# A Mamba scan and a mixture of experts on one core: the last chunk's serial stage in other PSUM banks, half of the scan's products on GpSimd, and activation tables requested by name

## What is computed

```python
# layer 0: Mamba block, then a small fp8 matmul
xi, res = split(x @ in_proj.T)                      # 256 + 256
xi = silu(causal_conv4(xi))
dt, B, C = split(xi @ x_proj.T, [64, 80])           # 64, 16, 16
delta = softplus(dt @ dt_proj.T + b)
h[t] = exp(delta*A) * h[t-1] + delta*B*u ; y = sum_n h*C + u*D    # 256 channels x 16 states
x = layernorm(x + (y * silu(res)) @ out_proj.T)
x = layernorm(x + fp8(x) @ fp8(w).T + bias)
# layer 1: a scan over 16 states with one step size per token, then the experts
x = layernorm(x + ssm(x))
probs = softmax(x @ Wr); top 2 of 8 experts, at most 512 slots for each expert
contrib = w * ((gelu(rms(x)@Wg[e]) * (rms(x)@Wu[e])) @ Wd[e] + x)    # 128 -> 256 -> 128
out = where(overflow, side_net(x) + x, x + sum(contrib)) ; x = layernorm(out)
```

## Time and profile before

| | us |
|---|---|
| median of 3 runs | 533.24 (530.87 to 534.29) |
| the profiled execution's own time | 535.09 |
| its span, first to last instruction | 533.3 |
| TensorE busy | 425.3 (80%) |
| VectorE busy | 419.7 (79%) |
| ScalarE busy | 315.1 (59%) |
| GpSimd busy | 178.6 (33%) |

### The profile page before, as it was taken

The page is one execution under the profiler, slowest core; times in us unless marked ns, Lnnn a source line. Parts: engine busy times, 40 slices in busy tenths (PEclk is TensorE's granted clock), DMA queues, the critical chain, the costliest instruction groups (busy, mean ns, idle before and its releaser), DMA issues.

```text
span 533.3 us, 5892 instructions
## 1 busy us (share of the span) xinstructions
PE 425.3 (80%) x1680; PEld 256.9 (48%) x1680; DVE 419.7 (79%) x942; ACT 315.1 (59%) x517; POOL 178.6 (33%) x147
## 2 busy tenths in 40 slices
PE   4976667699649999997569999775599995449994
PEld 3322212253235778552245776432367774147883
DVE  3087999997989999698989989978899884334654
ACT  2586552378738976577578785255787832544232
POOL 0056485555163434234163433451534100000000
PEclk9987977799969999999869999969799998656997
DMA  8295768666426354442193554620835000000000
GB/s 300 109 339 175 240 210 263 211 217 202 163 79 200 116 171 161 142 160 78 32 334 133 180 167 132 220 92 20 323 151 175 23 1 1 20 0 1 0 1 20
DMA packets 22064, 74.18 MB, mean 139 GB/s; under 512 B 2320, under 2 KB 4368, under 8 KB 21648
## 3 DMA queue, kind: packets, MB, share of 16 engines
q1 hardware_dynamic: 22032, 73.82, 41.0%
HBM read 72.50 MB, written 1.31 MB: 138 GB/s over the span
## 4 chain that ended last, share of the span: by engine, by line
PE 50%; DVE 21%; issue 13%; ACT 12%; POOL 2%; DVEq 0%; ACTq 0%; POOLq 0%
PE ps_y L475 12%; PE ps_u L608 9%; PE ps_g L564 8%; DVE ps_state L919 6%; PE ps_u L564 5%; DVE product L934 3%; PE ps_state L564 2%; ACT x L703 2%; ACT ps_state L692 2%; DVE stats L944 1%; PE ps_y L608 1%; POOL drive L813 1%; PE ps_g L523 1%; DVE l_state L990 1%; PE ps_g L534 1%
## 5 line engine op out<-in xcount | busy, mean ns | idle before, releaser
L813 POOL TENSOR_TENSOR drive<-du,b_row 128x512 f32<-128x512 f32 x128 | 164.0, 1290 | 208.3 <-DVE ps_state L919 186.0
L475 PE MATMUL ps_y<-product,par 128*128 128x512 f32 x256 | 135.7, 655 | 13.2 <-DVE product L934 12.9
L692 ACT ACTIVATE ps_state<-delta,decay_rate 128x512 f32<-128x512 f32 x128 | 86.2, 687 | 63.9 <-DVE product L934 61.9
L934 DVE TENSOR_TENSOR product<-ps_state,c_row 128x512 f32<-128x512 f32 x128 | 86.1, 680 | 5.5 <-PE ps_y L475 5.3
L919 DVE TENSOR_TENSOR_SCAN ps_state<-ps_state,carry,drive 128x512 f32<-128x512 f32 x64 | 81.5, 1282 | 4.0 <-ACT ps_state L692 4.0
L475 PEld LDWEIGHTS ps_y<-product,par 128*128 128x128 f32 x256 | 48.9, 208 | 70.6 <-issue 37.3
L919 DVE TENSOR_TENSOR_SCAN ps_state<-ps_state,drive 128x512 f32<-128x512 f32 x64 | 77.3, 1219 | 2.3 <-ACT ps_state L692 2.3
L608 PEld LDWEIGHTS ps_u<-wd,hidden 128*128 128x128 f32 x448 | 54.2, 191 | 5.4 <-issue 2.4
L608 PE MATMUL ps_u<-wd,hidden 128*128 128x128 f32 x448 | 54.6, 275 | 0.0
L1092 DVE SCALAR_TENSOR_TENSOR acc<-ps_u,net_weight,acc 128x128 f32<-128x128 f32 x128 | 35.9, 344 | 15.3 <-PE ps_u L608 12.5
L774 ACT ACTIVATE gelu<-ps_g 128x512 f32<-128x512 f32 (+1 forms) x42 | 24.4, 597 | 31.8 <-PE ps_g L564 18.5
(11 more groups left out here) (199 smaller groups left out, 605.4 us busy)
## 6 DMA issues: line engine op xcount, KB each, us to landing
b_row<-bc_dram SPq DMA_DIRECT2D x64, 512.0 KB, 5.0
c_row<-bc_dram SPq DMA_DIRECT2D x64, 512.0 KB, 4.1
x_in<-x_t SPq DMA_DIRECT2D x4, 256.0 KB, 7.0
gelu<-w_gate SPq DMA_DIRECT2D x1, 1024.0 KB, 9.3
hidden<-w_up SPq DMA_DIRECT2D x1, 1024.0 KB, 10.9
wd<-w_down SPq DMA_DIRECT2D x1, 1024.0 KB, 12.8
out<-result SPq DMA_DIRECT2D x4, 256.0 KB, 2.4
par<-params SPq DMA_DIRECT2D x1, 598.0 KB, 6.7
```

Of the source, the lines that this page charges most:

```text
L475: mm(ps_y[:, :], ident, product[:, g % PRODUCTS, :], start=False, stop=(n == STATE - 1)).then_inc(y_pe, 1)
L692: nc.scalar.activation(ps_state[g % RING][:, :], delta[:, c % 2, h, :], ACT.Exp, scale=decay_rate[:, h, n:n + 1]).then_inc(decay_act, 1)
L813: nc.gpsimd.tensor_tensor(drive[:, g % DRIVES, :], du[:, h, :], b_row[:, m % ROWS, n % 2, :], ALU.mult).then_inc(drive_pool, 1)
L934: v.tensor_tensor(product[:, g % PRODUCTS, :], state[:, :], c_row[:, m % ROWS, n % 2, :], ALU.mult).then_inc(product_dve, 1)
```

## The change

It does four things.

1. **Orders.** All lists of `PLACES` are new, one for each chunk, and gate, up and join are placed by half expert (17 places) in place of whole experts (9). On ScalarE and VectorE all 8 splits stand before the scan of chunk 0. VectorE's queue has, between the tail of chunk 0 (its step 1) and the first join of chunk 0, the units 1.4 to 1.21 (chunk.unit); in the MoE of chunk 0 1.22 to 2.4; then 2.5 to 2.12 before step 1 of chunk 1's tail; to its first join 2.13 to 2.28; in the MoE of chunk 1 2.29 to 3.10; then 3.11 and 3.12; and beside the tail of chunk 2 3.13 to 3.31, so all of the scan. On TensorE's queue two units of `finish` remain inside the MoE of chunk 2.
2. **Chunk 3's tail in the banks of the scan.** `tail_bank` gives chunk 3 `ps_state` and `ps_y`, and `l1_of` gives it `product` buffers for its temporaries. Its steps 0 to 11 are placed between the half experts of chunk 2's MoE on all engines. From step 12 (which overwrites the experts' input `hn_parts`) it waits for the last gate and up of chunk 2. `result` becomes an alias of `acc`, so the acc of a chunk is begun only when the result of the chunk before is stored.
3. **Products on GpSimd.** 10 units of chunk 0 (2, 5, ... 29) and the 16 odd units of chunks 1, 2 and 3 are `multiplied`: VectorE's scan writes to `drive` in SBUF in place of the PSUM bank, GpSimd multiplies there and, in chunks 0 and 2, copies the carry column. The bank is free for the next decay when the scan is done. `drive` goes from 5 to 6 buffers, `product` from 5 to 8. (Pairing of products by GpSimd is in the code, but its sets are empty.)
4. **Tables by name.** `use(name)` requests a set only where the set last requested in program order differs. By the new order that is 71 requests. The softplus of pre goes half by half through one `sp_exp` buffer.

The diff, cut to its core (the lists of places are left out; `tail_bank(c, ...)` replaces the banks in all of tail):

```diff
-DRIVES = 5
-PRODUCTS = 5
+DRIVES = 6
+PRODUCTS = 8
+THIRD = frozenset(range(2, UNITS, 3))
+ODD = frozenset(range(1, UNITS, 2))
+MULTIPLIED = (THIRD, ODD, ODD, ODD)
...
+        result = acc
...
+        def l1_of(c, name):
+            name = {"ln": "abs", "t": "sp"}.get(name, name)
+            i = L1_NAMES.split().index(name)
+            if c == CHUNKS - 1:
+                place = product[:, i, :]
...
+        def tail_bank(c, name):
+            if c == LAST:
+                return {"r1": ps_state[0], "x1t": ps_state[1], "ffn": ps_state[2], "x2t": ps_y, "dlt": ps_state[2],
+                        "bx": ps_state[0], "mean": ps_state[1], "r3": ps_y, "hnt": ps_state[2], "logits": ps_state[1],
+                        "counts": ps_y}[name]
...
# tensor
             def tail(c, k):
                 if k == 0:
-                    if c:
+                    if c == LAST:
+                        pe.wait_ge(product_dve, count(by_vector, STEPS - 1))
+                        pe.wait_ge(state_dve, STEPS)
+                    elif c:
...
             def gate(c, i):
                     if c == LAST:
-                        pe.wait_ge(product_dve, STEPS)
+                        pe.wait_ge(hidden_dve, 2 * NETS * c)
+                        pe.wait_ge(gelu_act, 2 * NETS * c)
...
# scalar
+            def use(name):
+                if table[0] != name:
+                    nc.scalar.preload_act_table_set(name)
+                    table[0] = name
...
             def step(c, k):
+                use(EXP_LN)
...
                 if old >= 0:
-                    act.wait_ge(product_dve, old + 1)
-                    if old // UNITS % PER_BATCH == 0:
-                        act.wait_ge(carry_dve, carries(old))
+                    if multiplied(old):
+                        act.wait_ge(state_dve, old + 1)
+                    else:
+                        made(act, old)
...
             def tail(c, k):
                 if k == 12:
+                    if c:
+                        act.wait_ge(gate_pe, 2 * NETS * c)
+                        act.wait_ge(up_pe, 2 * NETS * c)
...
                 if k == 15:
                     if c:
-                        after(act, fin_act, c - 1, "result")
+                        act.wait_ge(stored, 16 * c)
...
# gpsimd
             def step(c, k):
                 if g >= DRIVES:
-                    pool.wait_ge(state_dve, g - DRIVES + 1)
+                    if multiplied(g - DRIVES):
+                        made(pool, g - DRIVES)
...
+            def multiply(c, k):
+                if not multiplied(g):
+                    return
+                pool.wait_ge(state_dve, g + 1)
+                pool.wait_ge(c_in[m % ROWS], 16 * (m // ROWS + 1))
+                if g >= PRODUCTS:
+                    added(pool, g - PRODUCTS)
+                nc.gpsimd.tensor_tensor(product[:, g % PRODUCTS, :], drive[:, g % DRIVES, :], c_row[:, m % ROWS, n % 2, :],
+                                        ALU.mult).then_inc(product_pool, 1)
+                if c % PER_BATCH == 0:
+                    nc.gpsimd.tensor_copy(carry[:, h, n:n + 1], drive[:, g % DRIVES, CHUNK - 1:CHUNK]).then_inc(carry_pool, 1)
...
# vector
             def step(c, k):
-                v.tensor_tensor_scan(state[:, :], state[:, :], drive[:, g % DRIVES, :],
+                v.tensor_tensor_scan(drive[:, g % DRIVES, :] if multiplied(g) else state[:, :], state[:, :], drive[:, g % DRIVES, :],
...
             def finish(c, k):
+                if multiplied(g):
+                    return
```

More of the change, by code:

```diff
@@ L42 @@
 EXP_LN = "natural_log_exp_and_others"
+GELU = "gelu_and_others"
+SILU = "silu_and_others"
 PARAMS = {
@@ L203, in build @@
         product = sb("product", [P, PRODUCTS, CHUNK])
+        def l1_of(c, name):
[3 more added lines that the diff above has]
+                place = product[:, i, :]
+            elif i < 6:
+                place = gelu[:, i // 2, i % 2, :]
+            else:
+                place = hidden[:, 1, 0, :]
+            return place[0:STATE, :] if name in ("step", "decay", "drive") else place
         carry = sb("carry", [P, HALVES, STATE])
@@ L459, in pre @@
                     after(pe, pre_act, c, "low")
-                    last = mm(bank_[:, :], dt_proj[0:RANK, h * P:(h + 1) * P], low[0:RANK, q, :], start=True, stop=True)
+                    last = mm(bank_[:, :], dt_proj[0:RANK, h * P:(h + 1) * P], low[0:RANK, :], start=True, stop=True)
                 last.then_inc(pre_pe.sem, 1)
@@ L821, in tail, with pair @@
                                             ALU.add).then_inc(tail_pool.sem, 1)
-            run("gpsimd", du=make_du, step=step, tail=tail)
+            def multiply(c, k):
+                g = c * UNITS + k
+                h, n = divmod(k, STATE)
+                m = g // 2
+                if not multiplied(g):
[8 more added lines that the diff above has]
+                    nc.gpsimd.tensor_copy(carry[:, h, n:n + 1], drive[:, g % DRIVES, CHUNK - 1:CHUNK]).then_inc(carry_pool, 1)
+            def pair(c, k):
+                g = c * UNITS + k
+                if not paired(g):
+                    return
+                made(pool, g - 1)
+                made(pool, g)
+                nc.gpsimd.tensor_tensor(product[:, g % PRODUCTS, :], product[:, (g - 1) % PRODUCTS, :],
+                                        product[:, g % PRODUCTS, :], ALU.add).then_inc(pair_pool, 1)
+            run("gpsimd", du=make_du, step=step, multiply=multiply, pair=pair, tail=tail)
         @block.vector
@@ L993, in tail @@
+                    if not first:
+                        own(tail_dve, c - 1, "keep")
+                    do(tail_dve, v.tensor_tensor_scan(l1_state[:, :], l1_of(c, "decay"), l1_of(c, "drive"),
+                                                      0.0 if first else l1_carry[:, :], ALU.mult, ALU.add))
+                    own(tail_dve, c, "scan")
+                    do(tail_dve, v.tensor_copy(l1_carry[:, :], l1_state[:, CHUNK - 1:CHUNK]))
                 if k == 9:
                     after(dve, tail_pe, c, "r3")
-                    layer_norm_stats(tail_dve, c, lambda j: block_of(ps_g[0][:, :], j), "st3", "mo3")
+                    layer_norm_stats(tail_dve, c, lambda j: block_of(tail_bank(c, "r3")[:, :], j), "st3", "mo3")
```

347 lines of the change are left out of this document (188 added, 159 removed), and 113 rows, old and new, of the table PLACES.

## The result

| | kernel before | changed kernel |
|---|---|---|
| median (lowest to highest) | 533.27 us (530.87 to 534.29) | 486.97 us (484.33 to 489.31) |
| ratio to before, 95% interval | | 0.9137 (0.9084 to 0.9190) |
| profiled execution, span | 533.3 us | 485.43 us, 483.6 us |
| granted clock, mean of the span | 0.889 | 0.931 |

The changed kernel is faster by 46.3 us. The first three lines are from the page of the changed kernel: span, busy times, and the clock in 40 slices of 12.1 us. They answer to the earlier trace rows.

The account below looks back on a forecast made before the run. VectorE was taken to bound chunk 0's scan and the tails, TensorE the MoEs, latency chunk 3's tail. Chunk 3's first gate at 432 plus 55.4 gave 487, plus 1.8 gave 489, less 0.35% gave 488 us; range 472 to 520.

Parts of the forecast that it names:

- The overlap of chunk 3's tail: Chunk 2's MoE beside chunk 3's tail: 56 us, then 3 us of tail; chunk 3's first gate at 432 instead of 481.
- rival 1: Chunk 3's tail chain doesn't fit beside chunk 2's MoE; half of 31.8 us stays exposed: 504 us, chance 0.2.
- The last MoE: Chunk 3's MoE and the end: 52.4 us before, +3 for chunk 2's layer norm 4 and acc's wait; span ends at 487.
- The first scan: Chunk 0's scan: starts about 1 us earlier, GpSimd becomes the limit, 58 us; r1 (matmuls closing it) ends at 99, not 119.
- Chunk 0 to chunk 1: Between the ends of these chunks' scans: VectorE busy 108 us, 5 of it new contention; at 0.91 busy, 119 us.
- Chunk 1 to chunk 2: Between the ends of these chunks' scans: VectorE busy 90.7 us including 5 of contention; at 0.91 busy, 100 us.
- Chunk 2's tail: 19 units beside it in place of 14, a sum of 49 us, given 55 in place of 51; first join at 373.
- Products: 58 products leave VectorE (39.4 us) for GpSimd (75 us); carry copies 0.15 us each, writing the scan to SBUF nothing.
- Tables: 71 table loads in place of 65, +7.7 us of ScalarE, hidden under TensorE in chunk 0's MoE but with no room.
- rival 3: Table loads bound the first MoE and pre: 8 us there, 4 in chunk 1's MoE: 500 us, chance 0.12.
- rival 2: GpSimd and VectorE block each other, in the tails; all 72 two-input operations at 1.1 us: 555 us, slower, chance 0.07.
- Rival 4: Fewer products gain nothing in chunks 1 and 2's scans; only first scan and serial tail gain: 493 to 505, chance 0.06.

Follow-up runs that it names:

- e2: Changed kernel with steps 0 to 11 of chunk 3's tail placed after chunk 2's MoE on TensorE, ScalarE and VectorE: 514.68 us, ratio 0.9641.
- e4: Kernel before, with 58 more tile products on GpSimd into a tile nobody reads, nothing taken off VectorE: 543.70 us, ratio 1.0173.
- e8: Changed kernel with four more waits on GpSimd, holding its drive products of units 1.7, 1.16, 2.24 and 3.27 behind VectorE operations: 480.33 us, ratio 0.8987.
- e7: Changed kernel with the 16 odd products of chunk 0 on GpSimd in place of 10: 496.16 us, ratio 0.9294.
- e9: Changed kernel with the edits of e5 and e8 together: 480.95 us, ratio 0.9053.
- e12: Changed kernel with one more GpSimd wait: drive product of unit 1.7 after VectorE's shift in chunk 0's tail: 485.28 us, ratio 0.9144.
- e1: Changed kernel with all 128 products back on VectorE; orders, banks and tables as changed: 500.96 us, ratio 0.9376.
- e5: Changed kernel with ScalarE's gelus in chunk 0's MoE in 5 groups between the decays in place of 12: 485.73 us, ratio 0.9095.
- e6: Changed kernel with the table request points of the kernel before: 501.69 us, ratio 0.9386.
- e3: Changed kernel without any request for a table set: 528.17 us, ratio 0.9917.

## Why the prediction held, and where it didn't

**The overlap of chunk 3's tail.** Predicted: from the first join of chunk 2 to the first gate of chunk 3 56 us and 3; measured 50.2. The mechanism was right, TensorE at full clock with the tail's matmuls at their fast duration and 1 us of idle. The size was off by one step: I began the count of 39.4 us of MoE at the first join, but TensorE had begun with gates 5.4 us before it (378.2, 383.6). From first gate to first gate it is 55.6. This error gave back 9 us. The chain of some 20 hops fitted without exposing anything, so rival 1 did not occur; e2 shows what it is worth, 28 us.

**The last MoE.** Predicted 55.4 us, 3 more than before, for a layer norm that moved into it. Measured 49.8, 2.6 fewer. The layer norm cost nothing, and TensorE was at clock 0.92 there against 0.86 before. The first 12 us of this MoE, in the kernel before, e4, the changed kernel and e8:

```profile
481.00:493.00 12.00, 11.70 (x55) 9.17 (x56) 5.48 (x33) 5.07 (x10) 0.00 (x0) 0.63 0.01 1
492.40:504.40 12.00, 11.70 (x65) 9.45 (x66) 7.78 (x39) 5.24 (x11) 0.00 (x0) 0.86 0.00 1
434.00:446.00 12.00, 12.00 (x60) 9.44 (x60) 8.40 (x46) 9.30 (x15) 0.00 (x0) 0.86 0.08 23
429.40:441.40 12.00, 12.00 (x72) 9.82 (x72) 8.53 (x46) 10.60 (x19) 0.00 (x0) 1.00 0.08 23
```

The MoE lasts 52.4, 49.9, 49.8 and 48.3 us in them, in the order of the clock. e4 has the serial stage of the kernel before ahead of it, mostly at half of the clock, and the same clock and time as the changed kernel. So the 2.6 us are TensorE's clock, but that the change brought them is not shown: executions of the same stage differ by as much. The forecast was 5.6 us too long here: 3 were the term for the layer norm and the waits, which e4 (without that layer norm) and the changed kernel show to be nothing, and 2.6 are the clock, which was in no term.

**The first scan.** GpSimd as the limit was right (57.6 of 62 us busy; e7), and so was its price: 61.4 us from the first scan to the first of chunk 1, against 58. The start was wrong. I had the first scan 1 us earlier, and it came 1.7 later. VectorE's timeline just ahead of it:

```profile
32.55 1.64 DVE L1111 TENSOR_TENSOR delta<-sp_exp,delta 128x512 f32<-128x512 f32 x1
34.23 1.64 DVE L1113 TENSOR_TENSOR delta<-delta,sp_relu 128x512 f32<-128x512 f32 x1
35.90 1.64 DVE L1116 TENSOR_TENSOR delta<-delta,sp_abs 128x512 f32<-128x512 f32 x1
37.47 2.33 DVE L1127 TENSOR_TENSOR_SCAN ps_state<-ps_state,drive 128x512 f32<-128x512 f32 x2
```

The three operations take 0.69 us each where GpSimd is idle, and 1.64 here: with the softplus done half by half, GpSimd starts on the first half while VectorE does the second. That is 2.9 us of excess which I did not look for ahead of the scan. Beside it the start varies by itself: the first convolution's 16 matmuls take 8.90 us in this trace and 9.41 in that of before, but 7.14 or 7.15 in those of e2, e7 and e9, whose code is the same up to there, and in these the first scan comes at 35.6 to 35.8 with the same three long operations. Why is open; the granted clock is 1.00 in all of them. Together with the 3 us in the scan, r1 of chunk 0 is 6 us late; my limit for a wrong step was 108, and it was 105.1.

**Chunk 0 to chunk 1: the step that failed.** I had 119 us between the r1's, with 125 as the limit; it was 128.3. By the windows VectorE was busy for 56.7 + 45.0 + 12.5 = 114 us, where I had 108, and at 0.89 and not 0.91. Of the 6 us, 3.5 are the contention: 8.5 more than before, priced at 5. The counts were right (41 scans and 21 products between the points). The rest, 2 to 3 us, I can't assign: lost overlap is 1 us of it at most. What failed was not the total number of hits but that I took each hit as at most one operation of GpSimd. Of the 28.9 us of excess 4.6 are one instruction, and because a chain hung on it, it lengthened the stage by 3.2 us (e12). The bound that I gave, 1.1 us for an operation, doesn't hold.

The Trainium skill (SBUF — State Buffer, "Who interferes with whom") has VectorE and GpSimd share a port pair under an exclusive lock, with an instruction of two SBUF inputs on the losing side when GpSimd has begun. The trace agrees on who is hit by it: no scan and no product that reads PSUM is among the 31, and the MoEs, whose joins read PSUM, have an excess of 0. Three of the 31 have only one SBUF input: two `TENSOR_SCALAR` (1.40 and 1.47 us in place of 0.39) and a `CAST` (1.36 in place of 0.18). The wait can be longer than one GpSimd instruction: 4.77 us are four.

**Chunk 1 to chunk 2.** 100 predicted, 101.4 measured. VectorE was busy for 97.7 us where I had 90.7: 6.6 us of excess over that of before in place of 5 explain 1.6 of the 7, and fewer overlaps 3.5 (12.6 us of them against 16.1). It was idle for 4 us only in place of 9, which made up for it. So this number was right with both of its factors off.

**Chunk 2's tail.** From r1 of chunk 2 to the first join 55 predicted, 48.8 measured; I had added 6 us to a sum of 49 for the idle share of the stretch before. The sum alone was right.

**Products.** The prices held one by one: 1,287 ns against 1.27 to 1.29, 0.20 us for the copy (0.15 taken, 0.10 to 1.29 as bounds), nothing for the write to SBUF. The contention was under-priced, 17.5 us of excess against 12. The products' net is 14 us (e1), out of 39 us of VectorE's work.

**Tables.** The count of 71 was right, and that they are hidden under the first MoE: rival 3 had them bind there, and e5 and e9 show that they don't, though ScalarE is 93% busy. What I did not see is what the requests prevent. I set 71 against the 65 of before, and took the six as a cost of 7.7 us. In the new order the alternative was never 65; in the two runs without requests by name it was 82 (e6, 15 us) or 125 (e3, 41 us).

**Rivals 2 and 4.** GpSimd and VectorE did not block each other in the large: 0.93 us for each of 31 hits, where rival 2 had all 72 at 1.1. Rival 4 (no gain in chunks 1 and 2) is half true. From r1 of chunk 0 to r1 of chunk 1 the changed kernel takes 128.3 us for 41 scan units, before it took 113.6 for 32: what was gained up to r1 of chunk 0 (14.3 us) is given back, and r1 of chunk 1 ends where it did (233.4 and 233.0). But those 9 units are missing later, in the tail and MoE of chunk 2, where the gain returns.

**The sum of the errors.** Up to r1 of chunk 2 they are +6, +9 and +1 us, then -6 (chunk 2's tail), -9 (MoE of chunk 2) and -6 (last MoE): 483.6 for the span in place of 487, to 4 us. The median lies 1.5 us above the profiled execution, where I had it below, so that 488 against 487 looks closer still. The mechanisms behind it, overlap and GpSimd, are each shown by a run. The precision is luck.

## What to carry to other kernels

When work goes to GpSimd, list VectorE's instructions with two SBUF inputs that stand in a chain, and ask of each how many GpSimd instructions can be queued back to back at that moment, not whether one is running; a wait on GpSimd ahead of such a row costs it nothing where it has slack. Count the table loads of the alternative in the new order, not those of the old kernel. And when a stage is laid under another, count from the first instruction of the covering one. Before a microsecond or two in a stage is put down to the change, look at the same stage in a run that leaves it as it was: here the start and the last MoE moved by 2 us of themselves.

## What the runs showed of the hardware

- A VectorE instruction of 4 columns (0.15 us) took 4.77 us beside four GpSimd products back to back. At other places the two engines took turns: beside one row of GpSimd products, a chain of three VectorE instructions with two SBUF inputs took 1.64 us each in place of 0.69 (the earlier trace rows shows the same on two lines of the kernel before). Both outcomes are in the changed kernel. Its line of the `shift`, over the whole span (duration min/median/max in ns, first and last start):

```profile
L1163 DVE SCALAR_TENSOR_TENSOR shift<-moments,rstd x12: 149/162/4772, 108.9 to 479.1; 128x4 f32<-128x4 f32 x12
```

  What decides between the two outcomes stays open: no run here set out to vary it. The moment at which VectorE comes does not decide it alone: in e5 the same instruction came 0.20 us after the first of four products, as in the changed kernel, and ended with the first of them.

```profile
108.88 4.96 POOL L1010 TENSOR_TENSOR drive<-du,b_row 128x512 f32<-128x512 f32 x4
109.08 1.12 DVE L1174 SCALAR_TENSOR_TENSOR shift<-moments,rstd 128x4 f32<-128x4 f32 x1
```

- GpSimd pays less: its excess went from 2.3 to 8.9 us, on 1,329 ns mean for `drive` against 1,290.
- A switch of tables took 1.28 to 1.30 us, load and all, where one followed the other. ScalarE's timeline in the first MoE of the changed kernel:

```profile
168.07 1.28 ACT L782 ACT_TABLE_LOAD   x1
169.37 0.60 ACT L958 ACTIVATE gelu<-ps_g 128x512 f32<-128x512 f32 x1
169.98 1.28 ACT L782 ACT_TABLE_LOAD   x1
171.28 0.69 ACT L865 ACTIVATE ps_state<-delta,decay_rate 128x512 f32<-128x512 f32 x1
```

  The Trainium skill (ScalarE: Activation LUTs, "What ACT_TABLE_LOAD costs") gives 1,283 ns for the load, which the trace shows, and a drain of about 1,380 ns beside it, which it doesn't: the gelu starts 20 ns after the load ends.
- Without a request, Ln and Exp next to each other load a set each (e3): 125 loads in place of 71.
